# Edge counts per node: from a fifth block of the weighted one-hots' float32 products to a pair of float32r products per group

## What is computed

```python
messages = h_fwd[src] * direction[:, 0:1] + h_rev[src] * direction[:, 1:2]     # 50000 x 64
scores = leaky_relu(einsum('ef,hf->eh', messages, attn_forward[0]), 0.2)       # 50000 x 4
exp_scores = exp(scores - scores.max(axis=0, keepdims=True))
sum_exp = segment_sum(exp_scores, dst, num_segments=N)
norm = exp_scores / (sum_exp[dst] + 1e-10)
outs = [segment_sum(messages * norm[:, hd:hd + 1], dst, num_segments=N) for hd in range(H)]
```

```python
deg = segment_sum(ones_like(src), dst, num_segments=n)
agg = summed / maximum(deg, 1.0)[:, None]
```

## Time and profile before

| | us |
|---|---|
| median of 3 runs | 2693.89 (2690.0 to 2704.63) |
| profiled execution | 2691.82 |
| its span, first to last instruction | 2690.1 |
| stage 3 on TensorE, first products to the last group's start | 1259.0 to 1437.57 |
| TensorE busy / VectorE busy | 2428.9 / 1738.7 |
| mean granted clock of TensorE, share of 2.4 GHz | 0.936 |

### The profile page before, as it was taken

How to read it: one execution, slowest core, us unless ns; L and a number is a source line. 1 busy time by engine, 2 the same in 40 slices (tenths; PEclk the granted TensorE clock), 3 DMA queues, 4 the chain that set the end, 5 groups by cost and what they waited for, 6 DMA issues and landing times. The chain is left out here.

```text
span 2690.1 us, 46341 instructions
## 1 busy us (share of the span) xinstructions
PE 2428.9 (90%) x16026; PEld 2242.4 (83%) x16026; DVE 1738.7 (65%) x4274; ACT 1352.7 (50%) x2913; POOL 1244.5 (46%) x1402
## 2 busy tenths in 40 slices
PE   6888999899989998997999699966888999999998
PEld 6778998899988997996668688855778799998998
DVE  6666877678767776764656523246876677677565
ACT  4334656466545655555553322233234366665687
POOL 1323454245524551564876232245767377776000
PEclk9789999999999999999997599977989699999899
DMA  5211112111121111124223354536666076775011
GB/s 119 67 39 40 40 43 76 32 40 43 43 66 38 44 46 48 45 58 101 79 84 91 106 169 144 144 111 179 199 194 193 17 215 200 219 220 177 24 36 32
DMA packets 150284, 259.75 MB, mean 97 GB/s; under 512 B 35713, under 2 KB 95884, under 8 KB 149926
## 3 DMA queue, kind: packets, MB, share of 16 engines
q0 software_dynamic: 49632, 145.61, 19.9%
q1 hardware_dynamic: 100422, 111.17, 13.7%
HBM read 219.88 MB, written 36.82 MB: 95 GB/s over the span
## 5 line engine op out<-in xcount | busy, mean ns | idle before, releaser
L974 POOL DMA_INDIRECT gat<-table,srcT x400 | 414.2, 1036 | 352.9 <-DVE m L2820 230.3
L1129 POOL DMA_INDIRECT x_rows<-table,srcT x392 | 402.2, 1026 | 176.9 <-issue 122.7
L631 PE MATMUL pa<-w,act 128*125 128x256 f32 x2400 | 359.2, 288 | 13.0 <-DVE act L2579 12.8
L631 PE MATMUL pb<-hT,w 128*128 128x378 f32 (+1 forms) x1920 | 337.2, 312 | 1.8 <-DVE hT L2655 1.0
L631 PEld LDWEIGHTS pa<-w,act 128*125 128x125 f32 x2400 | 314.6, 187 | 17.7 <-DVE act L2579 17.6
L631 PEld LDWEIGHTS pb<-hT,w 128*128 128x128 f32 x1920 | 287.7, 190 | 4.1 <-DVE hT L2655 1.8
L2278 ACT ACTIVATE gf<-pb,bne 128x378 f32<-128x378 f32 (+1 forms) x320 | 193.9, 606 | 154.9 <-PE pb L631 143.5
L2579 DVE TENSOR_TENSOR act<-gf,act 128x378 fp32r<-128x378 f32 (+1 forms) x320 | 153.8, 483 | 106.7 <-ACT act L1996 104.9
L1993 ACT ACTIVATE gf<-pb,b1s 128x378 f32<-128x378 f32 (+1 forms) x320 | 165.6, 517 | 108.2 <-PE pb L631 98.3
L631 PE MATMUL pb<-xT,fw 128*128 128x378 f32 (+1 forms) x960 | 158.8, 316 | 0.0
L1996 ACT ACTIVATE act<-gf 128x378 fp32r<-128x378 f32 (+1 forms) x320 | 149.8, 468 | 10.1
(11 more groups left out here) (513 smaller groups left out, 5602.5 us busy)
## 6 DMA issues: line engine op xcount, KB each, us to landing
e<-in_L_ffn_W_dram SPq DMA_DIRECT2D x40, 512.0 KB, 4.1
spill<-m SPq DMA_DIRECT2D x80, 170.0 KB, 1.9
msg<-spill SPq DMA_DIRECT2D x40, 340.0 KB, 2.9
yslots<-yo SPq DMA_DIRECT2D x64, 128.0 KB, 2.0
fraw<-in_L_ffn_W_dram SPq DMA_DIRECT2D x32, 256.0 KB
w1r<-in_L_mix_W_dram SPq DMA_DIRECT2D x7, 1024.0 KB, 5.0
gat<-table,srcT POOLq DMA_INDIRECT x400
x_rows<-table,srcT POOLq DMA_INDIRECT x392, 3.7
```

The source lines that it names most:

```text
L631: mm = nc.tensor.matmul(ps, lhs(l), rhs(r), start=first and n == 0, stop=last and n == 2)
L974: pool.indirect_dma_start(out=gat[:, i % 2, c, :], out_offset=None, in_=table0, in_offset=bass.IndirectOffsetOnAxis(ap=srcT[:, i * GC + c: ...
L1129: pool.indirect_dma_start(out=x_rows[:, n % UB, c, :].bitcast(F32), out_offset=None, in_=table1, in_offset=bass.IndirectOffsetOnAxis(ap=sr ...
```

## The change

The one-hots move out of `ohx` into a tile of their own, `ohd`, in float32r. `ohx` keeps four blocks, so that the products of messages and weighted one-hots have 192 columns. The edge counts come from two products per group: 65 columns of ones (`ohd_one`, float32r) as weights, and the one-hots of the five even and of the five odd chunks (240 columns each) as moving data, added up in a bank of `pt`. VectorE adds each window's 48 counts to the last block of `acc` in an instruction of its own (semaphore `deg_used`), behind the window's add, and copies the ones once ahead of the first one-hots. GpSimd's 25 z adds are spread over the 40 groups, so that there is none in group 0.

```diff
--- before.py
+++ after.py
@@ -298,7 +298,9 @@
     xin = sb("xin", [TP, NT, D], F32, s3)
     ex = sb("ex", [P, NCH, MH], F32, s3)
     msg = sb("msg", [P, 2, CG, MW], F32, s3)
-    ohx = sb("ohx", [P, 2, CG, MH + 1, W], F32, s3)
+    ohx = sb("ohx", [P, 2, CG, MH, W], F32, s3)
+    ohd = sb("ohd", [P, 2, CG, W], R32, s3)
+    ohd_one = sb("ohd_one", [P, MF + 1], R32, s3)
     ohs = sb("ohs", [P, WS], F32, s3)
     iow = sb("iow", [P, WS], F32, s3)
     acc = sb("acc", [MF + 1, MH + 1, NP], F32, s3)
@@ -590,7 +592,7 @@
     for new, old, value in (("e_ld0", "wq_ld", 128), ("e_ld1", "bo_ld", 128), ("e_ld2", "wvo_ld", 128), ("e_ld3", "sm_ld", 320),
                             ("row2_st0", "row_st", 32 * NG + 16), ("row2_st1", "x_ld", 32), ("x_ld1", "p7_ld", 0), ("x_ld2", "p9_ld", 0),
                             ("x_ld3", "f_ld0", 0), ("x_ld4", "f_ld1", 0), ("be6_ld", "w_ld", 48),
-                            ("z_add", "tn_T", NL), ("z_ve", "cx_ps", NL), ("z_nr", "cx_go", NL), ("hot_w", "bq_ps", NL), ("b1_go", "bq_ev", NL),
+                            ("z_add", "tn_T", NL), ("z_ve", "cx_ps", NL), ("z_nr", "cx_go", NL), ("hot_w", "bq_ps", NL), ("b1_go", "bq_ev", NL), ("deg_used", "mo_ps", NL),
                             ("tab_go", "tn_go", NL), ("acc1_0", "ta_go", NL), ("xg_ld0", "gat0", 16 * GC * NCG), ("xg_ld1", "gat1", 16 * GC * NCG),
                             ("xg_T", "n_T", 3 * NG * NL), ("xg_up", "n_hi", 3 * NG * NL),
                             ("yo_go", "m_add", 3 * NG * NL), ("uw_ld0", "msg_st0", 16 * NCG), ("uw_ld1", "msg_st1", 16 * NCG), ("uw_ld2", "msg_ld0", 8 * NCG), ("yo_st0", "w1_ld", 48), ("yo_st1", "w2_ld", 64),
@@ -1049,7 +1051,7 @@
             for at in (slice(0, 4), slice(4, CG)):
                 cols = slice(n * CG + at.start, n * CG + at.stop)
                 k = at.stop - at.start
-                nc.gpsimd.tensor_tensor(ohx[:, n % 2, at, 0:MH - 1, :], ohx[:, n % 2, at, MH:MH + 1, :].to_broadcast([P, k, MH - 1, W]),
+                nc.gpsimd.tensor_tensor(ohx[:, n % 2, at, 0:MH - 1, :], ohd[:, n % 2, at, :].bitcast(F32).unsqueeze(2).to_broadcast([P, k, MH - 1, W]),
                                         ex[:, cols, 0:MH - 1].unsqueeze(3).to_broadcast([P, k, MH - 1, W]),
                                         ALU.mult).then_inc(s["wm_ready"], 1)
 
@@ -1059,8 +1061,8 @@
                 ones_column(n)
             if n == 0:
                 pool.wait_ge(s["xin_ld"], 32)
-            if n < NT:
-                me(nc.gpsimd.tensor_tensor(z[:, n, :], z[:, n, :], xin[:, n, :], ALU.add))
+            for t in range(n * NT // NCG, (n + 1) * NT // NCG):
+                me(nc.gpsimd.tensor_tensor(z[:, t, :], z[:, t, :], xin[:, t, :], ALU.add))
         me(nc.gpsimd.memset(tri[:, :, :], 1.0))
         me(nc.gpsimd.memset(um[:, :], 1.0))
         me(nc.gpsimd.memset(bnh[:, :, :], -0.5))
@@ -1552,8 +1554,15 @@
                 pe.wait_ge(s["ax_ready"], n * PR + q + 1)
                 if n:
                     pe.wait_ge(s["win_used"], (n - 1) * PR + q + 1)
+                if q == 0:
+                    if n >= 2:
+                        pe.wait_ge(s["deg_used"], past["deg_used"] + (n - 1) * PR)
+                    hots = ohd[:, b].rearrange("p (q k) w -> p q k w", k=2)
+                    for k in range(2):
+                        nc.tensor.matmul(pt[0:MF + 1, b, 0:PR * W].rearrange("p (q w) -> p q w", q=PR), ohd_one[:, :], hots[:, :, k, :],
+                                         start=k == 0, stop=k == 1)
                 for c in (2 * q, 2 * q + 1):
-                    last = nc.tensor.matmul(wbank[q][0:MF + 1, 0:(MH + 1) * W], msg[:, b, c, 0:MF + 1],
+                    last = nc.tensor.matmul(wbank[q][0:MF + 1, 0:MH * W], msg[:, b, c, 0:MF + 1],
                                             ohx[:, b, c].rearrange("p k w -> p (k w)"), start=c == 2 * q, stop=c == 2 * q + 1)
                 last.then_inc(s["win_ps"], 1)
         with pe.If(rest_flag(pe) == 1):
@@ -2175,7 +2184,7 @@
             act.wait_ge(s["oh_ready"], n + 1)
             for q in range(PR):
                 for c in (2 * q, 2 * q + 1):
-                    last = nc.scalar.mul(ohx[:, b, c, MH - 1, :], ohx[:, b, c, MH, :], ex[:, n * CG + c, MH - 1:MH])
+                    last = nc.scalar.mul(ohx[:, b, c, MH - 1, :], ohd[:, b, c, :].bitcast(F32), ex[:, n * CG + c, MH - 1:MH])
                 last.then_inc(s["ax_ready"], 1)
         stage_end(act, 3)
 
@@ -3015,7 +3024,7 @@
 
         def one_hots(n):
 
-            nc.vector.tensor_tensor(ohx[:, n % 2, :, MH, :], iota[:, 0:W].unsqueeze(1).to_broadcast([P, CG, W]),
+            nc.vector.tensor_tensor(ohd[:, n % 2], iota[:, 0:W].unsqueeze(1).to_broadcast([P, CG, W]),
                                     relT[:, n * CG:(n + 1) * CG].unsqueeze(2).to_broadcast([P, CG, W]),
                                     ALU.is_equal).then_inc(s["oh_ready"], 1)
 
@@ -3031,10 +3040,15 @@
                 dve.wait_ge(s["win_ps"], n * PR + q + 1)
                 if n * PR + q:
                     dve.wait_ge(s["win_used"], n * PR + q)
-                nc.vector.tensor_tensor(acc[:, :, bass.ds(at, W)], acc[:, :, bass.ds(at, W)],
-                                        wbank[q][0:MF + 1, 0:(MH + 1) * W].rearrange("p (k n) -> p k n", k=MH + 1),
+                nc.vector.tensor_tensor(acc[:, 0:MH, bass.ds(at, W)], acc[:, 0:MH, bass.ds(at, W)],
+                                        wbank[q][0:MF + 1, 0:MH * W].rearrange("p (k n) -> p k n", k=MH),
                                         ALU.add).then_inc(s["win_used"], 1)
-
+                if n * PR + q:
+                    dve.wait_ge(s["deg_used"], past["deg_used"] + n * PR + q)
+                degrees = acc[:, MH:MH + 1, bass.ds(at, W)].rearrange("p o n -> p (o n)")
+                nc.vector.tensor_tensor(degrees, degrees, pt[0:MF + 1, n % 2, q * W:(q + 1) * W], ALU.add).then_inc(s["deg_used"], 1)
+
+        me.link(dve, nc.vector.tensor_copy(ohd_one[:, :], ones[:, 0:MF + 1]))
         one_hots(0)
         for n in range(NCG):
             if n + 1 < NCG:
@@ -3045,6 +3059,7 @@
                 dve.wait_ge(s["act_go"], 2)
             add_windows(n, window_starts(n))
         dve.wait_ge(s["win_used"], NPR)
+        dve.wait_ge(s["deg_used"], past["deg_used"] + NPR)
         dve.wait_ge(s["act_go"], 2 + MH)
         dve.nop().then_inc(s["win_used"], PR)
```

## The result

The changed kernel took 2688.64 us, median of 20 runs (2676.79 to 2697.99); the kernel before, on the same chip, took 2696.71 (2686.92 to 2704.63). The ratio is 0.9971, with a 95% interval of 0.9959 to 0.9984: 7.8 us less, between 4.3 and 11.1. By the bound of 0.5% this is no change that a measurement tells, which was the likeliest case of the forecast; by its interval the time did fall. The forecast gain was 11.2 us.

What follows compares the result with a forecast made beforehand. The prediction took a two-group ring of hand-offs as the bound, 4.155 us a group falling to 3.885. Gains of 10.0, 0.9 and 0.35, together 11.2 us, gave 2680.6 for the profiled execution and 2683 for the median, range 2669 to 2700.

Steps and rivals of the forecast that it cites:

- the ring: Hand-offs among TensorE, VectorE and GpSimd over two groups in the first edge sums: 8.31 us before, 7.77 after.
- The main products: TensorE's products of messages and one-hots, 240 to 192 columns: pitch 0.202 to 0.163 us, 0.78 less a group.
- The degree pair: Two added float32r products a group on TensorE for the edge counts: 0.22 us, bounds 0.100 each and 0.81.
- The adds: VectorE's window add 0.353 us, degree add 0.208, windows 0.55 apart, one-hots 0.40 behind the last window add.
- VectorE's loop: VectorE's own work per group, four windows of 0.55 plus 1.54 to the next group: 3.74 us.
- The start of the stage: No z add in group 0: TensorE starts 0.68 us earlier; with about 0.3 in group 1, 0.9 gained.
- Elsewhere z adds lie in GpSimd's idle time: GpSimd's adds of `z` and `xin` after group 0 cost nothing; its work, 3.5 us a group, stays under 3.885.
- The sum: 37 groups at 0.27 us give 10.0, start 0.9, last group and end 0.35: together 11.2 us gained.
- (a): Rival: degree adds make VectorE the bound, windows 0.76 us, loop 4.58, total 2704 us; chance 0.11.
- (b): Rival: TensorE becomes the bound at 3.48 us a group, 25 us gained, total 2667; chance 0.10.
- (c): Rival: degree pair costs the float32 price, 0.81 us, group 4.18, only the start gained, total 2693; chance 0.17.
- (d): Rival: TensorE's clock falls as it idles more, a few groups at 6.9 us, total 2695 to 2710; chance 0.03.

Runs made afterwards that it cites:

- e9: Kernel before with third buffers, window starts of four groups read at a time and the one-hots' column numbers in PSUM; ratio 0.9974 to the kernel before.
- e12: Changed kernel with third buffers, window starts of four groups read at a time and column numbers in PSUM; 2671.2 us, ratio 0.991 to the kernel before.
- e10: Changed kernel without GpSimd's 25 z adds (sums of `z` and `xin`); ratio 0.9968 to the kernel before.
- e11: Changed kernel with the one-hots' column numbers read from a copy in PSUM, z adds kept; ratio 0.9954 to the kernel before.
- e5: Changed kernel with GpSimd's z adds put back into the first 25 groups, one each; ratio 0.9976 to the kernel before.
- e1: The kernel before, unchanged, run and profiled once more; ratio 0.9998.
- e4: Changed kernel with the one-hots and ones in plain float32 instead of float32r; ratio 0.9999 to the kernel before.
- e2: Changed kernel without VectorE's adds of the edge counts, degree products still made; ratio 0.9964 to the kernel before.
- e3: Changed kernel without degree products and without VectorE's adds of the edge counts; ratio 0.9935 to the kernel before.
- e7: Changed kernel with a third buffer for one-hots, weighted one-hots and messages, one-hots made two groups ahead; ratio 0.9947 to the kernel before.
- e6: Changed kernel with the window starts of four groups read at once; ratio 0.9949 to the kernel before.
- e8: Changed kernel with third buffers and the window starts of four groups read at once; ratio 0.9932 to the kernel before.

## Why the prediction was right, and where it was off

**The bound.** Right: the ring and not TensorE sets the pace, before and after. e9 confirms TensorE's 4.04 before (4.05) and e12 its 3.48 after (3.47); the lap without disturbance is 7.80 against 7.77. Without z adds in the way, half of what TensorE saved is kept by the ring (e10, e11); where two groups in a row have a z add another loop is the longer one, see below.

**The main products.** A pitch of (2.11 - 0.33) / 11 = 0.162 for 0.163. Right.

**The degree pair.** 3.47 - 20 x 0.1625 = 0.22 where TensorE runs without a pause, as taken; behind a pause the main products start 0.28 after the first degree record (1334.95 to 1335.23).

**The adds.** Window add 0.351 for 0.353, degree add 0.194 for 0.208, windows 0.56 apart for 0.55, the degree add 0.27 behind the window add's start. The one-hots come 0.39 behind the last window add (1338.78 to 1339.17) for 0.40. The overlaps of 0.08 that the earlier trace rows showed hold for the new instructions too. From the last add to the next group's first are 1.60, not 1.54: VectorE's loop is 3.84, not 3.74, still under 3.90.

**The start of the stage.** The 0.68 us came as forecast: between the wait for xin and TensorE's start of group 1 stood a z add and 1.94 us (1273.96 to 1275.90), now 1.26 (1271.02 to 1272.28), and 1.93 again in e5 (1275.02 to 1276.95). The 0.3 in group 1 can't be seen: from its start to that of group 2 took 5.77, before 5.54, and anything from 5.0 to 6.1 in the other runs with two buffers.

**The step that failed** is "Elsewhere z adds lie in GpSimd's idle time ... and are worth nothing either way". By GpSimd's time alone it is so, and the prediction's 3.5 for GpSimd's weighing, ones and z add is right. But the one-hots can't run beside the z add, so they belong into that sum, and it is 4.07 instead of 3.5 (e5), more than the ring's 3.90. In the kernel before, whose groups take 4.155, the same loop costs next to nothing: ten one-hots meet a z add there, none sooner than 0.57 us after its start, and none takes over 0.67 (in e1 two of eleven take more, 0.76 and 0.94). In the changed kernel they come early enough to fall on the z add, and where two groups in a row have one, the lap is 8.14 instead of 7.80. The Trainium skill states this in SBUF — State Buffer, "Who interferes with whom": a VectorE instruction with two SBUF inputs contends with a GpSimd instruction that reads SBUF, one with a single SBUF input does not. The trace agrees (0.99 over a z add; 0.647 with one operand in PSUM; window adds, which take one operand from PSUM, 0.351 in the mean). Its "fully blocks" comes within 0.14 us of what is seen, whichever of the two is second: blocked one-hots end 0.51 behind the z add and take 0.65 alone, blocked z adds end 0.58 behind the one-hots and take 0.72 alone. I had looked at whether the z adds fit, not at what their operands share with whom.

**The sum.** The pattern says 4.155 before and (4.07 + 4.07 + 3.73) / 3 = 3.957 after: 0.198 a group instead of 0.27, 7.3 us over 37 groups instead of 10.0. Of the missing 0.07, some 0.057 (3.957 - 3.90) are the exclusion, and 0.015 the ring's own 7.80 for 7.77. e10 and e11, which are free of it, have means 0.060 and 0.041 lower, which agrees, though one profile's mean is good for 0.05 only. Late groups cost as much after as before (2.1 and 2.4 us). The start gives 0.68. The end gives 0.61 where 0.35 was forecast: TensorE's first product behind the stage started 6.34 us after the last group's start, and 5.73 in the changed kernel. This makes 8.6, and 7.8 were measured. The number itself, 2683, was 5.6 off, and 2.8 of that lie in the base: the three runs shown had a median of 2693.89, and twenty have 2696.71.

**The rivals.** (a) Degree adds that take VectorE over: no, 0.56 a window. (b) TensorE as the bound: no, it is idle for 12 us of the stage; it becomes true only in e12. (c) No, but e4 shows that its price was right. (d) No: the granted clock is 1.00.

**Left open.** The long z adds of e2 and e3 are the same exclusion with the roles changed, since they all end a fixed time behind the one-hots; no kernel with one operand in PSUM was made of e2 or e3 to take it away. Nor is it shown what decides who goes first: where the one-hots started 0.24 us or more after a z add's start the z add always went first, up to 0.20 us after it the one-hots did, with a single exception at 0.19 (e7). The late groups (5.51, 5.12) waited for their messages: GpSimd's memset stood idle until the load had landed, for 1.36 us in the kernel before and 0.99 in e6. Why these loads are late is not shown.

Larger than all of this is the time behind stage 3. In the profiles the changed kernel's last group starts 11.0 us earlier than before, but the span is only 5.4 us shorter: from there to the end are 1252.5 us in the kernel before, 1255.3 in e1, 1256.3 in e9, and 1255.3 to 1263.6 in the eleven profiles with the change in them. The prediction had said that nothing behind the stage gives the gain back. The medians bear that out, as 7.8 of 8.6 us arrive, but three profiles against eleven can't exclude a small price, and no run looks for one.

## What to carry to other kernels

Find the ring before pricing the engine: a ring over two buffers takes an engine's time once in two groups, so here it kept half of what that engine saved. The same change was worth 7.8 us in the kernel as it was, and 17 to 21 with three buffers, wide loads and the column numbers in PSUM. When a cut lets stages move against each other, check what now runs side by side: on VectorE and GpSimd two elementwise instructions that each read two SBUF operands ran one after the other here, so their times belong into one sum. Moving one operand of VectorE's to PSUM ended it, and the instruction kept its 0.65 us.

## What the runs showed of the hardware

- A GpSimd add of two SBUF tensors (0.72 alone) and VectorE's comparison of two SBUF operands (0.65 alone) don't run side by side. Where VectorE's is second it ends 0.51 or 0.52 behind the add, and takes up to 0.99 over a z add (e5); where the z add is second it ends 0.58 or 0.59 behind the comparison, and takes up to 1.42 (e2). Over GpSimd's weighing the comparison takes mostly 0.8 to 1.3 (e8). With one operand from PSUM both keep their own lengths (0.647 and 0.724 to 0.729).
- So a loop in which GpSimd's add and VectorE's comparison follow each other counts both: 2.75 + 0.73 + 0.59 = 4.07 in each of e5's groups 3 to 24.
- A pair of float32r products of 240 columns costs TensorE 0.22 us (0.28 behind a pause), in float32 0.86: a factor of nearly four for twice the records.
